# Dense-expert stages of a six-stage layer: score products by tile, gate steps later, waits per half pair, the norm's scaling on ScalarE

## The chip, the core and the metric

The kernel runs on one core of a Trainium2 chip. The metric is the device time of one execution in microseconds (us), lower is better. The median of three runs is 1315.05 us (1312.03 to 1316.84). One execution was profiled: its own time is 1315.12 us, and the span from its first to its last instruction 1313.3 us. Engines are named as in the profile: PE is TensorE (PEld its weight loads), DVE is VectorE, ACT is ScalarE, POOL is GpSimd, SP the engine that issues most DMAs.

## The reference, cut to what matters

The input x has 2 x 2048 rows of 256 numbers. Six residual stages follow each other: a routed mixture of 32 experts, a gated linear attention, the mixture again, then the three that matter here: a dense-expert stage, a recurrent stage, and the dense-expert stage again with the same weights.

```python
x = x + 0.5 * L0_ffn(layernorm(x)); x = x + L0_attn(layernorm(x)); x = x + 0.5 * L0_ffn(layernorm(x))
x = x + 0.5 * L1_ffn(layernorm(x), router_w, w1, w2, w3)
x = x + L1_attn(layernorm(x), ...)
x = x + 0.5 * L1_ffn(layernorm(x), router_w, w1, w2, w3)

# L1_ffn: 8 experts of width 64, each row goes to its best 2
scores = x @ router_w.T
top, chosen = top_k(scores, 2); weight = softmax(top)
y = sum over the 2 of weight * ((silu(x @ w1[e]) * (x @ w3[e])) @ w2[e])
```

## The kernel before, in words

x stays in SBUF throughout, as 32 tiles of 128 rows. A dense-expert stage (`ffn1`, L1673; it is built twice, as ffn1a and ffn1b) does all 8 experts for all rows, 8 x 64 = 512 hidden columns, and multiplies each expert's hidden values by a gate that is zero for the experts not chosen. It works on 8 blocks of 4 tiles (512 rows). For a block, in this order:

- **norm**: `Norm.dve_moments` (L210) takes means and variances of 4 tiles on VectorE, `Norm.pool` (L239) makes the reciprocal deviation on GpSimd, `Norm.dve_apply` (L221) subtracts the mean and scales on VectorE (L229), `turn` (L1972) transposes eight 128x128 pieces on PE (L262), and ScalarE copies the result twice, as f32 (`turned`, L1861) and as bf16 (`turned16`, L1867).
- **score** (L1924): the router's product in f32, 8 columns wide, four tiles in one run (the trace has 16 matmuls for it), then `keep_logits` (L1873) on ScalarE.
- **gates** on VectorE (L1754): parts 0 and 1 find the largest scores and their places, 2 and 3 the difference and the one-hot rows, two `tanh` on ScalarE (L1901) the softmax of two, parts 4 and 7 to 10 the gate values, split in two bf16 halves. PE transposes them (`gates`, L1934), ScalarE copies them (L1896).
- **up** (L1942): for each quarter m of the hidden columns a pair of products, x w1 into `ps_a` and x w3 into `ps_b`, each two matmuls of 512 columns in bf16. Each of the two has a single PSUM bank. `keep_ab` (L1879) evicts both on ScalarE: silu of the first (L1883), a copy of the second (L1884). One semaphore, `ab_made`, tells that both halves are made, and one, `ab_kept`, that both are evicted.
- **spread** (L1953) brings the gate values of a quarter over all its columns, into `ps_c`. `hidden` on VectorE (L1802) multiplies silu by b (part 0, product m) and the result by the gates (part 1, h m).
- **down** (L1960): the output products of a half block, 8 matmuls; `add` (L1816) adds them into x on VectorE.
- ffn1a alone also has `combine`, passed from the mixture ahead: for each block and half VectorE adds three tables from DRAM into x (L1148, L1151) ahead of the block's norm. In ffn1b SP stores a finished block to the output.

The engines run lists written out by hand, tied by semaphores. `staged` (L115) makes rounds; in one round five blocks are in work at different steps: j2, j1, j0, je and jy, each one block behind the one before. je is in its up products, jy in its down products, j1 in its norm. PE's list in a round is

```python
gates(je); up(je, 1); spread(je, 0); down(jy, 0); up(je, 2); spread(je, 1); turn(j1); up(je, 3)
spread(je, 2); down(jy, 1); score(j1); spread(je, 3); up(j0, 0)
```

VectorE's list (L1822) begins with half a combine and the moments of j1, then has for m = 0 to 3 product m, the gate parts of j0, h m, with the scaling of j1 after h 0, an add in m = 1 and m = 3, and half a combine of j2 in m = 2. ScalarE's (L1886) is keep_ab 0, keep_logits(j0), the copy of je's gates, keep_ab 1, keep_ab 2, the tanh of j0, turned(j1), keep_ab 3, turned16(j1).

Of the kernel before, what the change touches and what calls it, by code (L numbers as in the profile page):

```python
# [1672 lines left out]
def ffn1(nc, name, x, con, w, weights16, combine=None, x_out=None):  # L1673
# [7 lines left out]
    with Scope(nc, name) as sc:  # L1681
# [10 lines left out]
        if first_use:  # L1692
# [14 lines left out]
        silu = sc.sb("silu", [P, NM1, BN], BF16)  # L1707
        prod = sc.sb("prod", [P, 2, BN], BF16)
        h = sc.sb("h", [P, 2, NM1, BN], BF16)
        names = ("router_landed landed cast logits_made logits_kept xb_made g_step diff_made part_made split_made "  # L1710
                 "g_turned g_kept ab_made ab_kept prod_made c_made h_made y_made y_added stored")
        (router_landed, landed, cast, logits_made, logits_kept, xb_made, g_step, diff_made, part_made, split_made,
         g_turned, g_kept, ab_made, ab_kept, prod_made, c_made, h_made, y_made, y_added, stored) = (
             sc.sem(n) for n in names.split())
        ln.xT_users = [(logits_made, 1), (xb_made, 1)]
# [6 lines left out]
        with nc.Block() as block:  # L1722
# [18 lines left out]
            @block.gpsimd  # L1741
            def _(pool):
                ln.pool_start()
                each(pool, ln.pool, NB)

            @block.vector
            def _(dve):
# [73 lines left out]

                def work(j2, j1, j0, je, jy):  # L1822
# [26 lines left out]
                if combine:  # L1849
                    combine.dve(number(0), 0)  # L1850
                    combine.dve(number(0), 1)
                ln.dve(number(0), tile_of(number(0)))
                if combine:
                    combine.dve(number(1), 0)
# [3 lines left out]
            def _(act):  # L1858
                s = nc.scalar

# [6 lines left out]
                def turned16(j):  # L1867
                    b, p, i = j
                    act.wait_ge(ln.transposed, b + 1)
                    after(act, ab_made, NM1 * (b - 1))  # L1870
# [8 lines left out]
                def keep_ab(j, m):  # L1879
                    c = NM1 * j[0] + m  # L1880
                    act.wait_ge(ab_made, c + 1)
                    after(act, prod_made, c + 1 - NM1)
                    s.activation(silu[:, m], ps_a[:], ACT.Silu)  # L1883
                    s.activation(b16[:, m], ps_b[:], ACT.Copy).then_inc(ab_kept, 1)  # L1884

                def work(j2, j1, j0, je, jy):  # L1886
                    for m in range(NM1):
                        if je:
                            keep_ab(je, m)
                        if m == 0:  # L1890
                            if j0:
                                keep_logits(j0)
# [4 lines left out]
                        if m == 2:  # L1897
# [10 lines left out]
                s.preload_act_table_set(SILU)  # L1908
                if first_use:
# [6 lines left out]
                turned(number(0))  # L1916
                turned16(number(0))
# [3 lines left out]
            def _(pe):  # L1921
                mm = nc.tensor.matmul

                def score(j):  # L1924
                    b, p, i = j
                    pe.wait_ge(ln.xT_ready, b + 1)
                    after(pe, logits_kept, b)
                    for t in range(BT):
                        for k in range(KD):
                            ins = mm(ps_r[:, t * E1:(t + 1) * E1], ln.xT[:, p, k, t * P:(t + 1) * P], wr[:, k, :],  # L1930
                                     start=k == 0, stop=k == KD - 1)
                    ins.then_inc(logits_made, 1)
# [498 lines left out]
```

## Time and profile before

| | |
|---|---|
| median of three runs | 1315.05 us |
| the profiled execution | 1315.12 us |
| its span | 1313.3 us |
| mean granted clock of PE | 0.875 |
| busy share of the span: PE, DVE, ACT, POOL | 84%, 58%, 39%, 29% |
| ffn1a, first instruction to the last | 881.1 to 1020.6 us |
| ffn1b, first instruction to the end | 1186.8 to 1313.3 us |

The two stages together take about a fifth of the span. The rest of this text looks at their rounds. A round is counted from one start of the gate transposes on PE (L1939) to the next; there are eight such starts in a stage. The granted clock (PEclk) is the share of PE's full clock that the chip let through: 1.00 is 2.4 GHz and 0.50 is 1.2 GHz, and a value between them is a mean over a stretch. In a timeline an entry in brackets tells how long the engine stood idle before the row, and which engine ended that.

### The profile page before, as it was taken

The page shows a single profiled execution, that of the slowest core. Times are in us where ns is not written, and L with a number is a line of the kernel's source. Part 1 is how long each engine was busy: PE and PEld are TensorE (multiplying, and loading weights), DVE is VectorE, ACT ScalarE, POOL GpSimd, SP SyncE. Part 2 cuts the span into 40 slices and gives each one's busy share as a digit, 9 for nine tenths or more (in the row PEclk, how much of TensorE's full clock was granted, in tenths as well). Part 3 has the DMA queues.
Part 4 walks back from the last instruction along what each step waited for, and adds up shares of the span by engine and source line. Part 5 has one row for each costly group of instructions (what it writes and reads, how often), then busy time and mean ns, then how long its engine had stood idle before and what let it go on. Part 6 is the DMA issues. An engine that isn't in the chain of part 4 may idle for free. (4 is left out here: it accounts for less than half of the span.)

```text
span 1313.3 us, 17356 instructions
## 1 busy us (share of the span) xinstructions
PE 1100.3 (84%) x5232; PEld 676.8 (52%) x5252; DVE 765.7 (58%) x2655; ACT 512.3 (39%) x989; POOL 383.5 (29%) x414
## 2 busy tenths in 40 slices
PE   7999898938999688887999797936888399987896
PEld 5756565614444355556656565614444255543443
DVE  4596352216664466665597352216996399965775
ACT  5421232304556544435422222314444455523543
POOL 3003656640000233323003647541000246521100
PEclk7699998969999799996699998966778699996878
DMA  8655757663230000003655647764320100000001
GB/s 287 213 171 143 147 126 181 147 133 125 97 96 0 9 1 0 0 0 119 213 171 140 143 94 185 171 126 161 111 82 1 42 1 0 0 0 1 33 32 65
DMA packets 102872, 123.70 MB, mean 94 GB/s; under 512 B 17264, under 2 KB 97504, under 8 KB 100704
## 3 DMA queue, kind: packets, MB, share of 16 engines
q1 hardware_dynamic: 87440, 100.54, 23.2%
q0 software_dynamic: 15360, 22.29, 11.2%
q8 instruction: 33, 0.54, 0.2%
q14 instruction: 39, 0.32, 0.1%
HBM read 73.53 MB, written 50.07 MB: 94 GB/s over the span
## 5 line engine op out<-in xcount | busy, mean ns | idle before, releaser
L614 POOL DMA_INDIRECT ffn_sums<-ffn0b_xT,ffn0b_into x40 | 62.8, 1571 | 45.0 <-ACT ffn0b_xT L890 31.2
L614 POOL DMA_INDIRECT ffn_sums<-ffn0a_xT,ffn0a_into x40 | 63.0, 1574 | 43.4 <-ACT ffn0a_xT L890 20.2
L1488 POOL TENSOR_TENSOR attn_attend_state_m<-attn_attend_state,attn_attend_heads 128x512 f32<-128x512 f32 x15 | 24.3, 1619 | 97.0 <-DVE attn_attend_state L1520 66.3
L1148 DVE TENSOR_TENSOR main_spare<-main_spare 128x512 f32<-128x512 f32 x32 | 22.0, 686 | 52.2 <-DMA main_spare<-ffn_sums 52.1
L1644 PE MATMUL attn_attend_ps_w<-attn_attend_wo,attn_attend_y 128*128 128x256 f32 x128 | 31.9, 392 | 20.8 <-DVE attn_attend_y L1531 20.8
L739 PE MATMUL ffn0b_ps_b<-ffn0b_early,main_x 128*128 128x160 f32 x256 | 44.6, 322 | 3.9 <-ACT ffn0b_early L873 3.2
L739 PE MATMUL ffn0a_ps_b<-ffn0a_early,main_x 128*128 128x160 f32 x256 | 44.0, 318 | 3.4 <-ACT ffn0a_early L873 2.5
L1520 DVE SCALAR_TENSOR_TENSOR attn_attend_state<-attn_attend_state,attn_decay,attn_attend_ps_s 128x256 f32<-128x256 f32 x32 | 14.0, 478 | 54.8 <-PE attn_attend_ps_s L1629 54.8
L2319 PE MATMUL attn_ps_r<-attn_xr,attn_wr 128*128 128x512 f32 (+1 forms) x96 | 45.2, 593 | 0.7 <-DVE attn_out L2183 0.7
L2314 PE MATMUL attn_ps_k<-attn_xk,attn_wk 128*128 128x512 f32 (+1 forms) x96 | 45.6, 597 | 0.0
L739 PEld LDWEIGHTS ffn0b_ps_b<-ffn0b_early,main_x 128*128 128x128 f32 x256 | 39.7, 203 | 9.4 <-issue 3.8
L761 PE MATMUL ffn0b_ps_b<-main_x,ffn0b_h 128*32 128x256 f32 (+2 forms) x144 | 44.1, 407 | 0.3 <-issue 0.3
L2329 PE MATMUL attn_ps_y<-attn_wv,attn_out 128*128 128x256 f32 (+1 forms) x192 | 43.0, 379 | 1.2 <-DVE attn_out L2183 1.2
L761 PE MATMUL ffn0a_ps_b<-main_x,ffn0a_h 128*32 128x256 f32 (+2 forms) x144 | 43.8, 406 | 0.0
L739 PEld LDWEIGHTS ffn0a_ps_b<-ffn0a_early,main_x 128*128 128x128 f32 x256 | 39.0, 200 | 8.9 <-issue 4.1
L1644 PEld LDWEIGHTS attn_attend_ps_w<-attn_attend_wo,attn_attend_y 128*128 128x128 f32 x128 | 23.0, 189 | 36.1 <-DVE attn_attend_y L1531 20.3
L2329 PEld LDWEIGHTS attn_ps_y<-attn_wv,attn_out 128*128 128x128 f32 (+1 forms) x192 | 36.3, 189 | 10.1 <-issue 3.3
L1033 DVE TENSOR_TENSOR ffn0b_h<-ffn0b_sg,ffn0b_ps_b 128x160 f32<-128x160 f32 x32 | 10.3, 321 | 53.2 <-ACT ffn0b_sg L880 43.8
L1508 DVE COPY_PREDICATED main_spare<-attn_attend_causal,attn_attend_ps_a 128x1024 f32<-128x1024 int32 x32 | 39.8, 1296 | 2.5 <-issue 2.5
L1883 ACT ACTIVATE ffn1a_silu<-ffn1a_ps_a 128x512 bf16<-128x512 f32 x32 | 19.1, 596 | 56.5 <-PE ffn1a_ps_b L1949 53.5
L1033 DVE TENSOR_TENSOR ffn0a_h<-ffn0a_sg,ffn0a_ps_b 128x160 f32<-128x160 f32 x32 | 10.3, 321 | 51.5 <-ACT ffn0a_sg L880 42.9
L1883 ACT ACTIVATE ffn1b_silu<-ffn1b_ps_a 128x512 bf16<-128x512 f32 x32 | 19.1, 596 | 50.5 <-PE ffn1b_ps_b L1949 47.8
(450 smaller groups left out, 2880.4 us busy)
## 6 DMA issues: line engine op xcount, KB each, us to landing
main_x<-w_experts SPq DMA_DIRECT2D x16, 1536.0 KB, 6.8
main_spare<-ffn_sums SPq DMA_DIRECT2D x96, 256.0 KB, 3.5
ffn_sums<-main_x SPq DMA_DIRECT2D x32, 512.0 KB, 5.3
ffn_rows<-ffn0a_early SPq DMA_DIRECT2D x8, 512.0 KB, 5.8
ffn_sums<-ffn0a_zero SPq DMA_DIRECT2D x8, 512.0 KB, 7.0
ffn_rows<-ffn0b_early SPq DMA_DIRECT2D x8, 512.0 KB, 2.9
ffn_sums<-ffn0b_zero SPq DMA_DIRECT2D x8, 512.0 KB, 6.3
x_out<-main_x SPq DMA_DIRECT2D x8, 512.0 KB, 2.9
```

The costliest lines, as they stand in the source:

```text
L614: g.indirect_dma_start(out=sums[:, :], out_offset=IndirectOffsetOnAxis(ap=into[:, at, j:j + 1], axis=0), in_=ys[:, n % NY, :], in_offset=N ...
L739: ins = mm(ps_b[:, p, j * CAP:(j + 1) * CAP], we[:, r, n, j, k * F:(k + 1) * F], xgT[:, k, e // ME % 2, e % ME].rearrange("p a b -> p (a b)"),
L761: ins = mm(ps_b[row:row + m, 2 + piece % 2, 0:D], eh[:, p, at:at + m], we[:, r, n, 2, :], start=True, stop=True)
L1033: v.tensor_tensor(eh[:, p, :], esg[:, p, :], ps_b[:, p, CAP:2 * CAP], ALU.mult).then_inc(eh_made, 1)
L1148: v.tensor_tensor(self.parts[:, half, 0], self.parts[:, half, 0], self.parts[:, half, 1], ALU.add).then_inc(self.added, 1)
L1488: g.tensor_tensor(state_m[:], state[:], heads[:].unsqueeze(1).to_broadcast([P, 2, D]), ALU.mult).then_inc(s_masked, 1)
L1508: vec.copy_predicated(att[:, p, s].rearrange("p (r n) i -> p r n i", n=2), causal[:].unsqueeze(1).unsqueeze(1).to_broadcast([P, 4, 2, P]), ...
L1644: ins = mm(ps_w[:, s, :], y[:, k, s, :], wo[:, k, :], start=k == 0, stop=k == KD - 1)
L1883: s.activation(silu[:, m], ps_a[:], ACT.Silu)
L2314: ins = mm(ps_k[0:rows, m % 2], wk[:, k, at:at + rows], xk[:, p, k, :], start=k == 0, stop=k == KD - 1)
L2319: ins = mm(ps_r[0:rows, m % 2], wr[:, k, at:at + rows], xr[:, p, k, :], start=k == 0, stop=k == KD - 1)
L2329: ins = mm(ps_y[:, t, :], out[0:rows, p, m, t * P:(t + 1) * P], wv[0:rows, m, :], start=m == 0, stop=m == NMH - 1)
```

## The change

- **Score by tile.** `score(j, t)` does one tile. PE's list becomes: gates(je), up(je, 1), spread(je, 0), score(j0, 3), down(jy, 0), up(je, 2), spread(je, 1), turn(j1), up(je, 3), spread(je, 2), score(j1, 0), down(jy, 1), score(j1, 1), spread(je, 3), up(j0, 0), score(j1, 2).
- **Gates later.** The fourth score tile of a block lies in the next round, so the gate parts are done at m = 1 (0, 1), m = 2 (2, 3) and m = 3 (4, 7, 8, 9, then 10).
- **Waits per half pair.** `ab_made` becomes `a_made` and `b_made`, and `a_kept` is added beside `ab_kept`: silu waits for its own half, and the first product of the next pair waits for silu alone.
- **Scaling on ScalarE.** `apply` does it as one activation per tile with a scale and a bias per row; GpSimd makes the bias (minus mean times scale) with two more operations per block, and sets a tile of -1 at the start. In a round it comes after keep_logits and ahead of keep_ab(je, 1).
- **Moments earlier.** VectorE takes the moments of j2, after h 2, and the combine halves of j2 come after h 0 and h 2.
- At the start of ffn1a the first block's norm comes ahead of the casts of the weights on ScalarE.

```diff
@@ gpsimd
-                each(pool, ln.pool, NB)
+                def norm(j):
+                    b, p, i = j
+                    pool.wait_ge(ln.moments_ready, b + 1)
+                    g.tensor_tensor(ln.ve[:, p, :], ln.moments[:, p, :, 1], ln.eps[:], ALU.add).then_inc(ln.ve_ready, 1)
+                    after(pool, shift_ready, b)
+                    g.tensor_tensor(neg_mean[:], ln.moments[:, p, :, 0], minus[:], ALU.mult)
+                    pool.wait_ge(ln.ve_ready, b + 1)
+                    after(pool, ln.xn_ready, b - 1)
+                    g.tensor_tensor(ln.rstd[:, p, :], ln.ve[:, p, :], ln.power[:], ALU.pow).then_inc(ln.rstd_ready, 1)
+                    pool.wait_ge(ln.rstd_ready, b + 1)
+                    g.tensor_tensor(shift[:, p, :], neg_mean[:], ln.rstd[:, p, :], ALU.mult).then_inc(shift_ready, 1)
+                each(pool, norm, NB)
@@ vector
                 def work(j2, j1, j0, je, jy):
-                    if j1:
-                        if combine:
-                            combine.dve(j1, 1)
-                        ln.dve_moments(j1, tile_of(j1))
                     for m in range(NM1):
                         if je:
                             hidden(je, m, 0)
-                        if m == 0:
-                            if je:
-                                hidden(je, m, 1)
-                            if j1:
-                                ln.dve_apply(j1, tile_of(j1))
                         if j0:
-                            for n in ((0, 1), (2, 3), (4,), (7, 8, 9))[m]:
+                            for n in ((), (0, 1), (2, 3), (4, 7, 8, 9))[m]:
                                 gates(j0, n)
                         if m == 3 and jy:
                             add(jy, 1)
                         if m == 3 and j0:
                             gates(j0, 10)
-                        if je and m:
+                        if je:
                             hidden(je, m, 1)
                         if m == 1 and jy:
                             add(jy, 0)
-                        if m == 2 and j2 and combine:
+                        if m == 0 and j2 and combine:
                             combine.dve(j2, 0)
+                        if m == 2 and j2:
+                            if combine:
+                                combine.dve(j2, 1)
+                            moments(j2)
@@ scalar
+                def apply(j):
+                    b, p, i = j
+                    act.wait_ge(shift_ready, b + 1)
+                    after(act, ln.transposed, b - 1)
+                    for t in range(BT):
+                        ins = s.activation(ln.xn[:, p, t, :], x[:, tile_of(j)(t), :], ACT.Identity,
+                                           scale=ln.rstd[:, p, t:t + 1], bias=shift[:, p, t:t + 1])
+                    ins.then_inc(ln.xn_ready, 1)
                 def keep_ab(j, m):
                     c = NM1 * j[0] + m
-                    act.wait_ge(ab_made, c + 1)
+                    act.wait_ge(a_made, c + 1)
                     after(act, prod_made, c + 1 - NM1)
-                    s.activation(silu[:, m], ps_a[:], ACT.Silu)
+                    s.activation(silu[:, m], ps_a[:], ACT.Silu).then_inc(a_kept, 1)
+                    act.wait_ge(b_made, c + 1)
                     s.activation(b16[:, m], ps_b[:], ACT.Copy).then_inc(ab_kept, 1)
...
                         if m == 0:
-                            if j0:
-                                keep_logits(j0)
                             if je:
                                 act.wait_ge(g_turned, je[0] + 1)
                                 after(act, c_made, NM1 * je[0])
                                 s.activation(gate_t[:], ps_g[:, 0:BN], ACT.Copy).then_inc(g_kept, 1)
-                        if m == 2:
+                            if j0:
+                                keep_logits(j0)
+                            if j1:
+                                apply(j1)
+                        if m == 2 and j1:
+                            turned(j1)
+                        if m == 3:
                             if j0:
...
                             if j1:
-                                turned(j1)
-                    if j1:
-                        turned16(j1)
+                                turned16(j1)
@@ tensor
-                    after(pe, ab_kept, c)
-                    for ps, wt in ((ps_a, w1), (ps_b, w3)):
+                    for ps, wt, kept, made in ((ps_a, w1, a_kept, a_made), (ps_b, w3, ab_kept, b_made)):
+                        after(pe, kept, c)
                         for k in range(KD):
                             ins = mm(ps[:], wt[:, k, m * P:(m + 1) * P], xb[:, p, k, :],
                                      start=k == 0, stop=k == KD - 1)
-                    ins.then_inc(ab_made, 1)
+                        ins.then_inc(made, 1)
```

## Rows read from the trace of the kernel before

**Rows 1.** Stretches by round; columns: us, busy (count) of PE, PEld, DVE, ACT, POOL; PEclk; DMA.

```profile
908.62:922.51 13.89, 12.20 (x48) 5.89 (x48) 8.84 (x39) 6.89 (x14) 0.11 (x1) 0.62 0.12 40
951.80:966.38 14.58, 13.56 (x64) 6.84 (x65) 13.20 (x54) 6.48 (x15) 1.29 (x2) 0.73 0.33 103
995.09:1007.62 12.53, 10.37 (x42) 3.99 (x41) 6.98 (x34) 5.41 (x13) 0.00 (x0) 0.73 0.00 0
1203.90:1217.86 13.96, 12.44 (x48) 5.89 (x48) 7.97 (x38) 7.00 (x14) 0.00 (x0) 0.62 0.00 1
1231.35:1244.29 12.94, 11.24 (x64) 6.23 (x65) 11.24 (x51) 6.88 (x14) 1.29 (x2) 0.89 0.22 74
1285.59:1295.50 9.91, 7.62 (x42) 3.24 (x41) 6.88 (x34) 5.41 (x13) 0.00 (x0) 1.00 0.13 45
```

**Rows 2.** Stretches around one fall of the clock, same columns.

```profile
1255.20:1258.60 3.40, 3.10 (x23) 2.17 (x24) 3.06 (x11) 1.11 (x2) 0.00 (x0) 1.00 0.18 60
1258.60:1262.00 3.40, 2.60 (x7) 0.72 (x8) 1.44 (x9) 1.87 (x6) 1.29 (x2) 0.50 0.28 95
```

**Rows 3.** Waits in ffn1b, 1203.9 to 1295.5: who, for whom, us in total, times, longest.

```profile
PE ffn1b_ps_a L1949 <- ACT ffn1b_b L1884: 7.6, 9, 0.9
```

**Rows 4.** Timeline, PE, upper level: start us, us taken, engine, line, operation, out<-in, count.

```profile
1252.85 0.59 PE L1949 MATMUL ffn1b_ps_a<-ffn1b_xb,main_w 128*128 128x512 bf16 x2
...
1253.81 0.38 PE L1958 MATMUL ffn1b_ps_c<-ffn1b_gate_t,main_pick 16*128 16x512 bf16 x1
...
1254.12 1.05 PE L1968 MATMUL ffn1b_ps_y<-main_w,ffn1b_h 128*128 128x256 bf16 x8
...
1255.01 1.85 PE L1930 MATMUL ffn1b_ps_r<-ffn1b_wr,ffn1b_ln_xT 128*128 128x8 f32 x16
...
1258.07 0.39 PE L1939 MATMUL ffn1b_ps_g<-main_ident,ffn1b_split 128*16 128x128 bf16 x4
...
1259.40 1.03 PE L1949 MATMUL ffn1b_ps_a<-ffn1b_xb,main_w 128*128 128x512 bf16 x2 [0.94 <-ACT ffn1b_b L1884]
```

**Rows 5.** Timeline, ACT: scaling in the recurrent stage; evictions in ffn1b.

```profile
1042.09 2.06 ACT L2256 ACTIVATE attn_ln_xn<-main_x,attn_shift,attn_ln_rstd 128x256 f32<-128x256 f32 x4
...
1258.26 0.60 ACT L1883 ACTIVATE ffn1b_silu<-ffn1b_ps_a 128x512 bf16<-128x512 f32 x1 [2.29 <-PE ffn1b_ps_b L1949]
1258.75 0.59 ACT L1884 ACTIVATE ffn1b_b<-ffn1b_ps_b 128x512 bf16<-128x512 f32 x1
1259.23 0.20 ACT L1876 ACTIVATE ffn1b_logits<-ffn1b_ps_r 128x32 f32<-128x32 f32 x1
```

**Rows 6.** Timeline, DVE: scaling, gates, products and moments in ffn1b.

```profile
1234.68 1.38 DVE L229 TENSOR_SCALAR ffn1b_ln_xn<-main_x,ffn1b_ln_moments,ffn1b_ln_rstd 128x256 f32 x4
...
1235.98 0.16 DVE L1762 MAX8 ffn1b_top<-ffn1b_logits 128x8 f32<-128x8 f32 x1
...
1236.93 0.42 DVE L1809 TENSOR_TENSOR ffn1b_prod<-ffn1b_silu,ffn1b_b 128x512 bf16<-128x512 bf16 x1
...
1241.80 0.18 DVE L1799 TENSOR_TENSOR ffn1b_split<-ffn1b_gate,ffn1b_split 128x32 bf16<-128x32 f32 x1
...
1257.82 1.40 DVE L213 BATCH_NORM_STATS2 ffn1b_ln_stats<-main_x 128x6 f32 x4
...
1259.35 0.28 DVE L218 BATCH_NORM_AGGREGATE ffn1b_ln_moments<-ffn1b_ln_stats 128x2 f32<-128x6 f32 x3
```

**Rows 7.** Timeline, DVE: half a combine in a round of ffn1a.

```profile
947.91 0.68 DVE L1148 TENSOR_TENSOR main_spare<-main_spare 128x512 f32<-128x512 f32 x1
...
949.64 0.42 DVE L1809 TENSOR_TENSOR ffn1a_prod<-ffn1a_silu,ffn1a_b 128x512 bf16<-128x512 bf16 x1
```

**Rows 8.** Timeline, PE, lower level (ffn1a's round and ffn1b's fill).

```profile
953.31 1.06 PE L1949 MATMUL ffn1a_ps_b<-ffn1a_xb,main_w 128*128 128x512 bf16 x2
...
954.30 0.60 PE L1958 MATMUL ffn1a_ps_c<-ffn1a_gate_t,main_pick 16*128 16x512 bf16 x1
...
1198.67 3.58 PE L1930 MATMUL ffn1b_ps_r<-ffn1b_wr,ffn1b_ln_xT 128*128 128x8 f32 x16 [1.42 <-ACT ffn1b_ln_xT L1865]
```

More of the change, by code:

```diff
@@ L1707, in ffn1 @@
         silu = sc.sb("silu", [P, NM1, BN], BF16)
+        minus = sc.sb("minus", [P, BT])
+        neg_mean = sc.sb("neg_mean", [P, BT])
+        shift = sc.sb("shift", [P, 2, BT])
         prod = sc.sb("prod", [P, 2, BN], BF16)
         h = sc.sb("h", [P, 2, NM1, BN], BF16)
[L1710 to L1713, printed above, removed]
+        names = ("router_landed landed cast minus_set shift_ready logits_made logits_kept xb_made g_step diff_made part_made split_made "
+                 "g_turned g_kept a_made b_made a_kept ab_kept prod_made c_made h_made y_made y_added stored")
+        (router_landed, landed, cast, minus_set, shift_ready, logits_made, logits_kept, xb_made, g_step, diff_made, part_made, split_made,
+         g_turned, g_kept, a_made, b_made, a_kept, ab_kept, prod_made, c_made, h_made, y_made, y_added, stored) = (
              sc.sem(n) for n in names.split())
-        ln.xT_users = [(logits_made, 1), (xb_made, 1)]
         wide = [P, BT, E1]
@@ L1820, in add, with moments @@
                     v.tensor_tensor(rows, ps_y[:], rows, ALU.add).then_inc(y_added, 1)
+                def moments(j):
+                    ln.dve_moments(j, tile_of(j))
                 def work(j2, j1, j0, je, jy):
-                    if j1:
-                        if combine:
-                            combine.dve(j1, 1)
-                        ln.dve_moments(j1, tile_of(j1))
                     for m in range(NM1):
@@ L1845, in work @@
                             add(jy, 0)
-                        if m == 2 and j2 and combine:
+                        if m == 0 and j2 and combine:
                             combine.dve(j2, 0)
[L1849 to L1854, printed above, removed]
+                        if m == 2 and j2:
+                            if combine:
+                                combine.dve(j2, 1)
+                            moments(j2)
+                for b in range(2):
+                    if combine:
+                        combine.dve(number(b), 0)
+                        combine.dve(number(b), 1)
+                    moments(number(b))
                 staged(dve, work, NB)
@@ L1869, in turned16 @@
                     act.wait_ge(ln.transposed, b + 1)
-                    after(act, ab_made, NM1 * (b - 1))
+                    after(act, b_made, NM1 * (b - 1))
                     s.activation(xb[:, p], ps_t[:], ACT.Copy).then_inc(xb_made, 1)
@@ L1903, in work @@
                             if j1:
[L1904 to L1906 removed]
+                                turned16(j1)
                 s.preload_act_table_set(SILU)
+                act.wait_ge(ln.power_set, 1)
+                apply(number(0))
+                turned(number(0))
+                turned16(number(0))
                 if first_use:
@@ L1922, in _, with score @@
                 mm = nc.tensor.matmul
-                def score(j):
+                def score(j, t):
                     b, p, i = j
[L1926 to L1932, printed above, removed]
+                    if t == 0:
+                        pe.wait_ge(ln.xT_ready, b + 1)
+                        after(pe, logits_kept, b)
+                    for k in range(KD):
+                        ins = mm(ps_r[:, t * E1:(t + 1) * E1], ln.xT[:, p, k, t * P:(t + 1) * P], wr[:, k, :],
+                                 start=k == 0, stop=k == KD - 1)
+                    if t == BT - 1:
+                        ins.then_inc(logits_made, 1)
                 def gates(j):
@@ L1980, in work @@
                         spread(je, 0)
+                    if j0:
+                        score(j0, 3)
                     if jy:
@@ L1990, in work @@
                         spread(je, 2)
+                    if j1:
+                        score(j1, 0)
                     if jy:
@@ L1993, in work @@
                     if j1:
-                        score(j1)
+                        score(j1, 1)
                     if je:
@@ L1998, in work @@
                         up(j0, 0)
+                    if j1:
+                        score(j1, 2)
                 warm(nc, con, ps_t[:, 0, :], 5 if combine else 3)
@@ L2002, in _ @@
                 pe.wait_ge(router_landed, 16)
-                score(number(0))
+                for t in range(BT - 1):
+                    score(number(0), t)
                 if first_use:
```

5 lines of the change are left out of this document (3 added, 2 removed).

## The prediction

> **What bounds the kernel now.** Only the two dense-expert stages are touched, so I read them round by round, with the stretches view cut at the start of each round's gate transposes on TensorE (PE, L1939) [rows 1]. From the first to the seventh of these starts ffn1a takes 995.09 - 908.62 = 86.5 us and ffn1b 1285.59 - 1203.90 = 81.7 us; the seventh round takes 12.5 and 9.9. In a round of ffn1a VectorE is busy 13.20 of 14.58 us, so VectorE (DVE) is nearly the bound there. In ffn1b it is busy 11.24 of 12.94 in the round with the highest clock, and ScalarE (ACT) has half its time free: 6.88 us. The same view in short stretches shows the clock [rows 2]: PE runs at its upper level (1.00, 2.4 GHz) through 1255.20 to 1258.60, a stretch filled mostly by the narrow score matmuls, then waits, and the next stretch is at the lower level (0.50, 1.2 GHz). So a round has a mean granted clock of 0.62 to 0.89 [rows 1], and PE's own work takes long. Last, the waits: PE stood 7.6 us, nine times, for the copy of the second projection [rows 3], 0.94 us once in the timeline [rows 4].
>
> **What a round is afterwards.** I follow one round from the start G of its gate transposes, PE at the upper level. On PE come: transposes 0.39, expert pair 1 0.96 (1252.85 to 1253.81), spread 0 0.31, the fourth score tile 1.85 / 4 = 0.46 [rows 4]: 2.12 us. ScalarE has by then evicted what it could, but its list now reads: keep the logits, scale four tiles of the next block, and only then evict pair 1. The copy of logits takes 0.20, silu starts 0.49 before the copy of b, which takes 0.59 [rows 5]. The scaling does not exist in these stages; the same instruction on the same shapes, with a scale and a bias per row, stands in the recurrent stage: 2.06 us for four [rows 5]. I take that; below it the nearest row is VectorE's own 1.38 [rows 6], above it nothing longer than 4 x 0.60 = 2.4 (a silu of twice the columns, rows 5). So the pair is in SBUF at 2.12 + 0.20 + 2.06 + 0.49 + 0.59 = 5.46 us, and VectorE's product 1 waits for it. VectorE has done h 3, product 0 and h 0 by about 2.4, and in its list stands nothing else (in ffn1a half a combine): **some 3 us idle per round, where the scaling was meant to relieve it.**
>
> From product 1 on VectorE's list is unbroken. Its length can be read off: from product 1 to the end of the last gate step the round before does exactly these instructions in 1241.80 + 0.18 - 1236.93 = 5.05 us; added to them are gate parts 0 and 1, now behind product 1, 1236.93 - 1235.98 = 0.95, and the moments of the block two ahead, now behind h 2, 1259.35 + 0.28 - 1257.82 = 1.81 [rows 6]. Sum 7.81. The last gate step is what the next G waits for, so a round is at least 5.46 + 7.81 = **13.3 us in ffn1b**. In ffn1a half a combine stands behind h 2 as well, 949.64 - 947.91 = 1.73 [rows 7]: **15.0 us**. The round before with the highest clock was 12.94, and the usual one of ffn1a 14.58 [rows 1].
>
> **The parts, priced.** (1) VectorE loses 1.38 us of scaling per round [rows 6]; it buys nothing inside the chain, because the idle 3 us take its place. (2) The waits per half pair: silu can start a half pair earlier, and PE's next first half needs silu alone. In the rounds this is covered, since what is late next is ScalarE's scaling. PE after the fourth score tile and four output products (0.89 [rows 4]) is at 3.01, and pair 2 may start at 2.12 + 0.20 + 2.06 + 0.60 = 4.98: **PE stands 2.0 us**, against 0.94 before [rows 4]. It pays in the drain of a stage, where no scaling is queued: three waits of 0.9 [rows 3] fall to some 0.25 each, 2.0 us per stage, 4.0 in all. (3) The score tiles cost the same, 4 x 0.46, but lie between wide products. (4) GpSimd gets two small operations more per round; it is busy 1.29 of 14.58 us [rows 1], and the shift, started when the moments end, some 2.6 us ahead of G, is wanted 2.3 us behind it: cover of 3 us, cost nothing. SP issues the same loads and stores; the first half combine moves ahead of the gates of its round, so its next load starts earlier; nothing. (5) The fill of ffn1b: scaling costs 0.7 more than on VectorE (2.06 against 1.38) and waits for one more GpSimd operation, 0.3; and block 1's scaling now sits behind the last score tile of block 0, where VectorE did it beside the scores: about 1.6. Together +2.6, an estimate, bounds 1 and 4. In ffn1a the first block's turn no longer stands behind the weight casts, which gives the same amount back: 0, bounds -2 and +2.
>
> With the clock always at the upper level: round 1 has no output adds (12.1 and 13.8), rounds 2 to 5 are 13.3 and 15.0, round 6 has no moments but PE's own list and stand, 12; round 7 has no scaling, 9.7. ffn1b rounds 1 to 6: 12.1 + 53.2 + 12 = 77.3, -4.4; ffn1a: 13.8 + 60.0 + 12 = 85.8, -0.7; round 7: -0.2 and -2.8; fill +2.6, drains -4.0. Sum **-9.5 us**.
>
> **The clock.** Will it stay up? PE's list takes about 10 us of the 13.3. The thin stretches are now two: the fourth score tile and the stand of 2.0 with only output products between, and, at the round's end, the third score tile and a wait of 1.3 for the gates (PE is through at about 11.9). Before, one thin stretch (1.85 of scores, 0.94 of waiting [rows 4]) was enough to lose the upper level in nearly every round. I take it that the level still falls in most rounds. Where it falls ahead of the scaling, pair 1 takes 0.99 per half instead of 0.48, the tile 3.58 / 4 = 0.90 instead of 0.46 [rows 8]: chain +1.6, and both later spreads come late, up to 1.7 more. Where it falls behind the stand, pairs 2 and 3 make h 1 and h 2 late by 0.7 and 0.8: +1.5. With three rounds in ten spared I take +1.5 on average for the twelve rounds 1 to 6, +18, and +3 for the first rounds, which begin at the lower level (0.62 [rows 1]), and ffn1a's seventh. So -9.5 + 21 = **+11.5 us**. Most of it is in ffn1a, the rest in ffn1b.
>
> The profiled execution took 1315.12 us, 1.8 more than its span of 1313.3, and the median of three is 1315.05; the sum is made against the former: 1326.6.
>
> **Where a rule speaks otherwise.** VectorE is busy 91% of a ffn1a round [rows 1]. The Trainium skill (Perfetto Trace Analysis, Optimizing Scalar/DVE Operations) says that where VectorE is saturated, moving work to ScalarE may make sense. By that rule the 1.38 us would come off each of 14 rounds.
>
> **Rivals.** *The upper level holds.* For it: no narrow stretch is longer than 0.46 us, and rounds of the drain with waits of 0.9 ran at 1.00 (9.91 us, [rows 1]). Against it: the stand of 2.0. Time: the sum above, 1305.6. It decides if PE's stand after the first output products leaves the granted clock at 1.00. Chance 0.17.
> *The relief counts.* VectorE's list, not the wait behind the scaling, sets the round: 14 x 1.38 = 19.3 less, fill +2.6: 1298. It needs product 1 to be ready when h 0 ends; the order on ScalarE speaks against it. That is the result the page's rule would give. Chance 0.06.
> *Both halves cancel.* The level falls in every second round only and the wait costs 0.8 instead of 1.5: -9.5 + 10 = 1316. Chance 0.15.
> *The lower level stays.* PE stands a quarter of each round and is not given the upper level again: every product, transpose and tile doubles, and PE's list alone makes rounds of some 18 us: 12 x 4.5 = 54 more, -9.5 + 54 = +44.5, 1360. Against it: behind the stand lie some six microseconds of unbroken wide work, and the round [rows 1] always got the level back before. Chance 0.05.
> My forecast, slower by the queue on ScalarE with a clock that still falls: 0.57, own range 1318 to 1342.
>
> **How the numbers follow.** A measurement of this kernel tells about 0.5%, 6.6 us, from no change: 1308.5 to 1321.6. Faster: most of the first rival and the second, 0.17. Same: the rest of it, the third, and the low end of the forecast, 0.27. Slower: the rest, 0.56. The range 1304 to 1342 takes in the first rival and leaves out the second and fourth and the forecast's tail.
>
> **What would show it.** Right: VectorE's product waits for ScalarE's b some 3 us in each round; PE's first half of pair 2 waits about 2 us for silu; gate transposes wait for the split, VectorE; rounds of 14 to 15.5 us in ffn1b, 16 to 17.5 in ffn1a; PEclk still alternating; the drains 2 us shorter. Wrong: rounds under 13.3 and 15.0 (then the chain is misread), or PEclk at 1.00 throughout, or a wait of VectorE for DMA.

## The result and the profile after

The kernel after takes 1345.22 us (median of four, 1341.36 to 1350.33), the kernel before, run beside it, 1314.03: ratio 1.0235, 95% interval 1.019 to 1.028, **slower by some 31 us**. The forecast was 1326.6 and its range ended at 1342. The profiled execution took 1341.36 us. Its page, the clock line of the 40 slices included:

```profile
span 1337.5 us, 17455 instructions
...
PE 1106.0 (83%) x5252; PEld 684.8 (51%) x5252; DVE 745.0 (56%) x2591; ACT 548.4 (41%) x1053; POOL 388.7 (29%) x448
...
PEclk7699899969999799986799899766678699996788
```

The rounds in the stretches view, cut as in [rows 1]; columns: busy us of PE, its weight loads, VectorE, ScalarE, GpSimd, each with its instructions; then the granted clock, the DMA share, GB/s. First the six rounds of ffn1a and of ffn1b as one stretch each, then a middle and the seventh round of ffn1a and three rounds of ffn1b:

```profile
903.58:1011.67 108.09, 85.71 (x369) 46.19 (x368) 66.46 (x277) 54.82 (x109) 8.23 (x20) 0.68 0.19 59
1220.96:1311.74 90.78, 74.63 (x369) 42.14 (x368) 52.64 (x247) 54.71 (x109) 8.23 (x20) 0.77 0.07 24
...
959.01:978.51 19.50, 15.61 (x65) 8.16 (x65) 11.93 (x50) 9.31 (x18) 1.70 (x4) 0.66 0.25 80
1011.67:1021.08 9.41, 8.20 (x45) 3.57 (x44) 7.00 (x35) 5.50 (x13) 0.00 (x0) 1.00 0.01 2
1253.63:1268.64 15.01, 12.68 (x64) 7.27 (x65) 9.37 (x44) 9.20 (x18) 1.61 (x4) 0.77 0.11 37
1268.64:1281.98 13.34, 10.12 (x64) 6.05 (x64) 9.01 (x44) 9.09 (x18) 1.70 (x4) 1.00 0.12 39
1281.98:1298.03 16.05, 12.96 (x65) 7.18 (x65) 9.29 (x44) 9.31 (x18) 1.61 (x4) 0.79 0.10 33
```

VectorE has less work than before (11.9 busy in a round of ffn1a against 13.2 in [rows 1]) and the rounds are longer, 19.5 against 14.6. Six rounds of ffn1a took 86.5 us and take 108.1, of ffn1b 81.7 and 90.8. Over the two stages, each from its first instruction: ffn1a +18.5 (fill +0.6, six rounds +21.6, the seventh -3.1, drain -0.6), ffn1b +10.0 (fill +2.9, rounds +9.1, the seventh -0.5, drain -1.5). Between them the recurrent stage is 1.3 longer, and the unchanged stages ahead were 5.7 shorter in this execution. Together 24.2, the difference of the two spans (1337.5 and 1313.3).

Now the timeline of one round of ffn1b (start, length, engine, line, what it does; in brackets the idle time ahead and what ended it). It answers to [rows 4 to 6]:

```profile
1253.63 0.39 PE L1969 MATMUL ffn1b_ps_g<-main_ident,ffn1b_split 128*16 128x128 bf16 x4 [1.09 <-DVE ffn1b_split L1817]
...
1255.24 0.61 PE L1959 MATMUL ffn1b_ps_r<-ffn1b_wr,ffn1b_ln_xT 128*128 128x8 f32 x4
...
1255.89 0.20 ACT L1900 ACTIVATE ffn1b_logits<-ffn1b_ps_r 128x32 f32<-128x32 f32 x1 [1.24 <-PE ffn1b_ps_r L1959]
1256.13 2.08 ACT L1881 ACTIVATE ffn1b_ln_xn<-main_x,ffn1b_shift,ffn1b_ln_rstd 128x256 f32 x4
1258.11 0.58 ACT L1907 ACTIVATE ffn1b_silu<-ffn1b_ps_a 128x512 bf16<-128x512 f32 x1
1258.58 0.58 ACT L1909 ACTIVATE ffn1b_b<-ffn1b_ps_b 128x512 bf16<-128x512 f32 x1
...
1258.74 1.03 PE L1979 MATMUL ffn1b_ps_a<-ffn1b_xb,main_w 128*128 128x512 bf16 x2 [1.16 <-ACT ffn1b_silu L1907]
1259.19 0.43 DVE L1827 TENSOR_TENSOR ffn1b_prod<-ffn1b_silu,ffn1b_b 128x512 bf16<-128x512 bf16 x1 [3.16 <-ACT ffn1b_b L1909]
```

ScalarE ends its wait for the fourth score tile at 1255.89, copies the logits, scales for 2.08, and only then evicts pair 1, whose products were done before the tile. Product 1 starts 5.56 us after the gate transposes; VectorE had stood 3.16. The waits view of ffn1a's rounds (engine, line waited for; us in total, times, longest), to be read against [rows 3]:

```profile
DVE ffn1a_h L1832 <- PE ffn1a_ps_c L1988: 24.4, 18, 2.5
DVE ffn1a_prod L1827 <- ACT ffn1a_b L1909: 16.7, 8, 3.4
...
PE ffn1a_ps_g L1969 <- DVE ffn1a_split L1817: 13.4, 5, 2.8
...
PE ffn1a_ps_a L1979 <- ACT ffn1a_silu L1907: 8.9, 6, 2.8
```

The second and fourth lines are the forecast's waits. The first and third are its surprise in size: PE stands 2.7 us ahead of the gates in ffn1a, where before it stood once in six rounds, for 0.6; and VectorE waits again and again for a PE that runs mostly at its lower level, 24.4 us in 18 waits where before it waited 5.1 in 6.

### The profile page after: what moved, and what is told of

It reads as the page before. It is cut to its first block and busy times, and to the rows that moved or that the text cites. A ratio compares the mean times of both kernels' runs of the same rounds, so it can differ in the third digit from the quotient of the medians.

```text
span 1337.5 us, 17455 instructions
## 1 busy us (share of the span) xinstructions
PE 1106.0 (83%) x5252; PEld 684.8 (51%) x5252; DVE 745.0 (56%) x2591; ACT 548.4 (41%) x1053; POOL 388.7 (29%) x448
## 5 line engine op out<-in xcount | busy, mean ns | idle before, releaser
L614 POOL DMA_INDIRECT ffn_sums<-ffn0b_xT,ffn0b_into x40 | 62.9, 1572 | 45.0 <-ACT ffn0b_xT L890 19.7
L2210 DVE TENSOR_TENSOR_SCAN attn_st<-attn_keep,attn_carry,attn_kr 128x512 f32<-128x512 f32 (+1 forms) x24 | 33.1, 1381 | 7.9 <-ACT attn_kr L2311 7.8
L1832 DVE TENSOR_TENSOR ffn1a_h<-ffn1a_prod,ffn1a_ps_c 128x512 bf16<-128x512 bf16 x32 | 21.9, 685 | 27.3 <-PE ffn1a_ps_c L1988 27.2
```

Of the source, the lines that this page charges most:

```text
L614: g.indirect_dma_start(out=sums[:, :], out_offset=IndirectOffsetOnAxis(ap=into[:, at, j:j + 1], axis=0), in_=ys[:, n % NY, :], in_offset=N ...
L2210: v.tensor_tensor_scan(st[0:rows, m % 2], keep[0:rows, m:m + 1].to_broadcast([rows, BN]), kr[0:rows, m % 2], carry[0:rows, p, m:m + 1], AL ...
```

## Experiments

The times are medians, and the ratios are to runs of the kernel before beside them, with a 95% interval. What each is about: the queue on ScalarE (first, second, fourth, seventh), the clock (third, eighth, eleventh), the parts alone (fifth, sixth, ninth), the best of both (tenth, twelfth). Six rounds of a stage are quoted as one stretch each, ffn1a above, ffn1b below.

No edit touches what runs ahead of ffn1a. Yet ffn1a starts between 874.6 and 884.5 us in the fourteen profiled executions, so a time of the whole kernel carries some microseconds from there. The last column leaves them out: in the one profiled execution of each kernel, the time from ffn1a's first instruction to the end, which is the two dense-expert stages and the recurrent stage between them. The others of its executions have no trace, so how far that column varies by itself is not known.

| kernel | median | ffn1a starts | from there to the end |
|---|---|---|---|
| before | 1314.03 | 881.1 | 432.2 |
| after | 1345.22 | 875.5 | 462.0 |
| 1, scaling behind pair 1 | 1314.55 | 883.0 | 429.8 |
| 2, combine and moments first | 1311.33 | 874.6 | 428.3 |
| 3, both stands filled | 1319.9 | 880.8 | 441.2 |
| 4, both orders | 1293.7 | 877.9 | 413.5 |
| 5, waits alone | 1292.9 | 880.4 | 407.5 |
| 6, tiles alone | 1300.06 | 880.2 | 418.0 |
| 7, scaling on VectorE | 1313.84 | 882.3 | 431.1 |
| 8, fill ahead of pair 2 | 1331.17 | 879.9 | 451.8 |
| 9, waits and tiles | 1286.37 | 875.4 | 411.9 |
| 10, each stage its order | 1290.88 | 876.2 | 410.6 |
| 11, fill ahead of the gates | 1331.3 | 880.7 | 449.5 |
| 12, scaling on ScalarE on the ninth | 1300.17 | 884.5 | 417.0 |

**1. The scaling behind pair 1.** On the kernel after, ScalarE's work:

```diff
+                        if m == 1:
                             if j0:
                                 keep_logits(j0)
                             if j1:
                                 apply(j1)
```

> The changed kernel, with keep_logits and the scaling on ScalarE put behind the eviction of pair 1 (before that of pair 2). Queue theory (the scaling ahead of pair 1 makes VectorE idle 3 us and PE stand 2 us in each round): product 1 no longer waits, PE's wait for silu before pair 2 falls from 1.2 or more to under 0.5 us, the upper-level chain falls from 13.3 and 15.0 us to about 12 and 13.7 us, and the time to 1295 to 1315. Rival (the moments and the combine half behind h 2 are what makes the rounds long, the queue is covered): the round stays over 14.5 and 17, and the time within 0.5% of the changed kernel's 1345, 1338 to 1352.

1314.55 us, ratio 0.998 [0.9945, 1.0015]: 31 us less than after, the whole of its loss, for the place of five operations in one queue (the copy of the logits and four scalings). In the last column it is 32. PE still stands 2.7 us ahead of ffn1a's gates here, and the clock there is 0.72.

```profile
911.30:1005.69 94.39, 78.92 (x364) 45.62 (x369) 66.34 (x277) 55.63 (x109) 8.21 (x20) 0.72 0.22 68
1214.46:1288.28 73.82, 65.20 (x363) 39.66 (x368) 52.51 (x247) 54.49 (x109) 8.22 (x20) 0.87 0.09 29
```

**2. Combine and moments ahead of product 1.** On the kernel after, VectorE's idle 3 us are given work; a wait for the shift two blocks earlier comes with it.

```diff
-                        if m == 0 and j2 and combine:
-                            combine.dve(j2, 0)
-                        if m == 2 and j2:
+                        if m == 0 and j2:
                             if combine:
+                                combine.dve(j2, 0)
                                 combine.dve(j2, 1)
+                            dve.wait_ge(shift_ready, j2[0] - 1)
+                            v.memset(waiter[:], 0.0)
                             moments(j2)
```

> The changed kernel, with both combine halves and the moments of j2 on VectorE behind h 0 (m = 0), where it idles, instead of behind h 2. Queue theory: they fill the idle time, which is about 3 us; the chain behind product 1 loses 1.8 us in ffn1b and 3.5 in ffn1a, of which 2.1 come back in ffn1a since the three take longer than the idle time; rounds of about 12 and 13.6 us at the upper level, time 1297 to 1322. Rival (VectorE's list is not what the gates wait for; PE's list at the lower level is): gates no longer wait for the split, but the rounds shorten by less than 1 us, and the time is over 1330.

1311.33 us, ratio 0.9974 [0.995, 0.9998]. The profiled execution, at 1305.52, was the fastest of its ten. There ffn1a gained most: six rounds fell from 108.1 to 83.8.

```profile
903.21:987.02 83.81, 66.28 (x364) 38.17 (x369) 65.71 (x282) 54.75 (x109) 8.07 (x20) 0.89 0.24 76
1197.26:1276.60 79.34, 65.77 (x364) 38.99 (x369) 53.44 (x252) 54.24 (x109) 8.51 (x20) 0.88 0.08 27
```

**3. PE's two stands filled.** On the kernel after, six wide products of no use ahead of the gate transposes and eight ahead of pair 2, in the rounds that have both blocks:

```diff
+                    if je and j0:
+                        pe.wait_ge(xb_made, j0[0] + 1)
+                        fill(6)
                     if je:
                         gates(je)
...
                         down(jy, 0)
+                    if je and j0:
+                        fill(8)
                     if je:
                         up(je, 2)
```

> The changed kernel, with matmuls that compute nothing needed (512 columns, bf16, into the free transpose bank) put in PE's two stands: 6 ahead of the gate transposes, 8 ahead of pair 2. It prices the clock by itself. Clock theory (rounds over 13.3 and 15.0 us are the lower level's doing): granted clock at 1.00 in nearly all rounds, rounds of 13.3 to 14 in ffn1b and 15.0 to 15.7 in ffn1a, time 1306 to 1320. Rival (the excess is something else, such as waits that the chain left out): the clock rises, the rounds stay at 15 and 18, time over 1335. A third way: the filler is late itself, lengthens PE's list at the lower level, and the time rises.

1319.9 us, ratio 1.0038 [1.0017, 1.0059].

```profile
910.15:1000.53 90.38, 80.63 (x445) 44.75 (x453) 66.13 (x277) 54.32 (x108) 8.24 (x20) 0.94 0.22 70
1214.97:1294.94 79.97, 76.95 (x445) 42.47 (x452) 51.90 (x247) 54.32 (x108) 8.24 (x20) 0.99 0.09 30
```

PE does more and the kernel is 25 us faster than after. Cut at the gates, rounds 2 to 5 of ffn1b are 13.4 each at a clock of 1.0, those of ffn1a 15.0 at 1.00 and 16.0 at 0.89: the chain without the clock, 13.3 and 15.0, was read rightly. The fall of the clock costs the kernel after some 25 us or more (21 by the last column), since the fill takes time too (the seventh rounds grow by 1.3 each). Ahead of ffn1a's gates the six products fill only part of the stand: 1.4 to 1.5 us of 2.7 are left.

**4. Both orders (1 and 2) at once.**

> The edits of e1 and e2 together. Queue theory: the edits treat the same idle time, so they do not add up: with nothing idle VectorE's list (some 10 us in ffn1b, 13.2 in ffn1a) and PE's list of 10 set the round: 11 to 12.5 and 13.5 to 14.5 us, time 1285 to 1308, below the kernel before. Rival (each removes a stand of its own): the gains against the changed kernel add up. If the clock keeps falling in each round, both gains shrink and the time stays over 1315.

1293.7 us, ratio 0.9818 [0.9768, 0.9868].

```profile
906.30:995.81 89.51, 79.65 (x363) 46.59 (x368) 65.87 (x282) 55.85 (x109) 8.06 (x20) 0.72 0.23 71
1204.88:1266.08 61.20, 57.52 (x363) 36.03 (x369) 51.82 (x252) 53.66 (x109) 8.07 (x20) 0.99 0.11 35
```

In ffn1b PE is busy 57.5 of 61.2 us: it hardly stands, and the clock stays up. ffn1a did not follow (89.5 at 0.72): there VectorE does both halves of a combine and the moments ahead of product 1, and PE's spreads wait for h, 8.0 us in five waits. That order on VectorE alone is not the cause: the tenth has it too, and its ffn1a took 83.1. Why the two orders together do badly in ffn1a stays open.

**5. The waits per half pair alone**, on the kernel before. ScalarE's half is shown; PE waits for `a_kept` ahead of a pair's first product and for `ab_kept` ahead of its second.

```diff
-                    act.wait_ge(ab_made, c + 1)
+                    act.wait_ge(a_made, c + 1)
                     after(act, prod_made, c + 1 - NM1)
-                    s.activation(silu[:, m], ps_a[:], ACT.Silu)
+                    s.activation(silu[:, m], ps_a[:], ACT.Silu).then_inc(a_kept, 1)
+                    act.wait_ge(ab_made, c + 1)
```

> The kernel before with the waits per half pair alone; score tiles in one run, scaling, gates and moments on VectorE as before. Prediction: in the rounds nothing, because silu's half pair is covered there; only the drains lose PE's stands for the copy of b, 2.0 us per stage, so about -4 us against before, and after's own drains (12.4 in both stages against 13.0 and 13.8) ask for -2. A rival, that the waits also shorten PE's stand of 0.94 in each round and with it save the upper level: 12 rounds x 0.5 or more, 1300 to 1308 us and PEclk at 1.00 in more rounds than one.

1292.9 us, ratio 0.9838 [0.9807, 0.9869]: 21 us, and I had given the part 4. The rival on record was nearer, and still too small: it gave 1300 to 1308.

```profile
907.35:990.32 82.97, 70.72 (x363) 38.34 (x368) 73.74 (x301) 42.45 (x84) 6.58 (x11) 0.82 0.26 81
1195.07:1264.06 68.99, 61.45 (x364) 35.41 (x369) 60.07 (x271) 40.99 (x84) 6.58 (x10) 0.94 0.10 32
```

Beside the kernel before, whose clock over these six rounds was 0.71 and 0.75, PE's stand of 0.9 behind the scores is gone and the clock is 0.82 and 0.94. So the part acts in the rounds. In ffn1b's six rounds before, those stands were 5.7 us, and the rounds are 12.7 shorter: the rest goes with the clock.

**6. The score tiles alone**, on the kernel before, all four within the same round:

```diff
+                    if j1:
+                        score(j1, 0)
                     if jy:
                         down(jy, 1)
                     if j1:
-                        score(j1)
+                        score(j1, 1)
                     if je:
                         spread(je, 3)
+                    if j1:
+                        score(j1, 2)
                     if j0:
                         up(j0, 0)
+                    if j1:
+                        score(j1, 3)
```

> The kernel before with its score products dealt out one tile at a time between wide work of the same round; everything else as before. If the run of 1.85 us of narrow products is what loses the upper level in the round before, the clock stays at 1.00 in most rounds and the rounds shrink to VectorE's own list, 12.5 to 13 us: some 1300 us. If the stand of PE is enough by itself, the clock stays at 0.7 to 0.75 and the time within 5 us of before. I take the second, 0.6 to 0.4, since the gates now wait longer: the last tile, and with it the logits, comes later by the tiles' distance.

1300.06 us, ratio 0.9884 [0.9851, 0.9916]. My bet lost again: the tiles cost the same and win 14 us.

```profile
907.43:994.23 86.80, 74.86 (x364) 42.76 (x369) 73.55 (x301) 42.20 (x85) 6.78 (x11) 0.77 0.26 78
1201.65:1271.72 70.07, 64.85 (x363) 37.77 (x369) 59.50 (x271) 41.33 (x85) 6.59 (x10) 0.89 0.09 31
```

**7. The scaling back on VectorE**, on the kernel after, behind h 0:

```diff
+                        if m == 0 and j1:
+                            ln.dve_apply(j1, tile_of(j1))
...
                                 keep_logits(j0)
-                            if j1:
-                                apply(j1)
```

> The kernel after with the four scaling operations back on VectorE, behind h 0, and nothing else changed (GpSimd still makes the shift, unused). My account of the round says that pair 1 is then in SBUF at 2.12 + 0.20 + 0.49 + 0.59 = 3.4 and VectorE, through with h 0 at 2.4, scales until 3.8, so the chain is 3.8 + 7.81 = 11.6 us in ffn1b and 13.3 in ffn1a, 1.7 less than after per round: 13 x 1.7 = 22 less, and PE's stand ahead of pair 2 falls from 2.0 to some 0.3, so the clock gives back more: 1305 to 1318 us. If the loss of after were in the later gates and moments, or in the score tiles, and not in the scaling's place on ScalarE, the time stays over 1335.

1313.84 us, ratio 0.9989 [0.9967, 1.0011], in the range given. The first block's scaling goes back with the others. Two rounds of ffn1b at a clock of 0.98 and 1.00 took 11.5 and 11.4 us, where the chain says 11.6. ffn1a stays at 0.72: its first five rounds are 15.8 to 17.0, not 13.3, and PE still stands 2.7 to 2.9 ahead of the gates.

```profile
908.49:1004.40 95.91, 80.39 (x362) 46.27 (x369) 73.65 (x301) 42.69 (x84) 8.65 (x22) 0.72 0.22 69
1209.31:1287.70 78.39, 70.47 (x364) 41.52 (x369) 59.85 (x271) 42.41 (x85) 8.21 (x20) 0.81 0.08 27
```

**8 and 11. One stand filled at a time**, on the kernel after: experiment 3 with the eight products ahead of pair 2 alone, and with the six ahead of the gates alone.

> The kernel after with eight wide products of no use ahead of pair 2, in the rounds of both stages, and none ahead of the gate transposes (the earlier run had both). It tells which stand loses the upper level. If the stand of 2.0 ahead of pair 2 is what loses it, PEclk is 1.00 or nearly in ffn1b with rounds of 13.4, and ffn1a at 15 to 16: 1320 to 1326. If the stand ahead of the gates (1.1 in ffn1b, 2.7 in ffn1a) loses it too, ffn1b is as with both and ffn1a keeps 0.7 and rounds of 17 to 18: about 1333. If the gates' stand is the cause in both stages, the time stays at 1340 or more.

> The kernel after with six wide products of no use ahead of the gate transposes, and none ahead of pair 2: the counterpart of the run with those ahead of pair 2 alone (1331.2), both together gave 1319.9. If either stand alone is enough to lose the upper level, the two halves of the fill do not add up to the whole: 1330 to 1342 here, ffn1a with rounds of 16 to 19 and a clock of 0.7 to 0.8. If the two stands' costs add, 1345 - (25 - 14) = 1334, with rounds of 16.5 in ffn1a. If the gates' stand was the larger part of it in ffn1a (2.7 us there), ffn1a's clock is over 0.85 and its rounds are near 15.5: about 1330 with ffn1b still at 15 to 16.

1331.17 us, ratio 1.0119 [1.0083, 1.0154], and 1331.3, 1.0118 [1.0068, 1.0167]: each 14 of the 25 us, but in different stages. First the former, then the latter:

```profile
908.29:1010.91 102.62, 88.09 (x410) 48.06 (x416) 66.42 (x277) 53.95 (x109) 8.23 (x20) 0.77 0.20 62
1221.53:1305.50 83.97, 76.30 (x410) 43.15 (x416) 52.24 (x247) 53.93 (x109) 8.24 (x20) 0.89 0.08 26
```

```profile
910.27:1003.11 92.84, 71.33 (x399) 40.67 (x405) 65.81 (x277) 54.60 (x108) 8.24 (x20) 0.93 0.22 68
1214.75:1304.41 89.66, 75.68 (x398) 42.55 (x404) 52.53 (x247) 55.08 (x108) 8.24 (x20) 0.87 0.08 28
```

With the gates' stand filled in part (1.4 to 1.5 of 2.7 us are left) ffn1a goes from 0.68 to 0.93 and loses 15.3 us of 108.1; with pair 2's filled it loses 5.5. In ffn1b it is the other way: 1.1 against 6.8. With pair 2's filled, three rounds of ffn1b ran at 1.00 with stands of 1.1 to 1.3 us ahead of the gates. The eleventh run also has a round of ffn1a whose clock was 1.00 throughout, with the other stand in it (stretches, then PE's timeline):

```profile
926.77:941.97 15.20, 11.38 (x69) 6.49 (x70) 11.74 (x50) 9.09 (x18) 1.91 (x6) 1.00 0.34 109
```

```profile
932.20 0.60 PE L1979 MATMUL ffn1a_ps_a<-ffn1a_xb,main_w 128*128 128x512 bf16 x2 [2.29 <-ACT ffn1a_silu L1907]
```

So a stand of 2.29 us ahead of pair 2, with one of 1.50 ahead of the gates, did not lose the level in that round. It took 15.20, where the chain says 15.0.

**9. Both parts that won alone** (5 and 6 together, on the kernel before).

> The kernel before with both parts that won alone: waits per half pair (-21 us against before) and score tiles dealt out one at a time within the round (-14). If both work through the same thing, a clock that stays up once the thin stretch of narrow products and standing is shorter, they cannot add in ffn1b, whose rounds are near 11 us in both and at 0.90 to 1.00: 1285 to 1293 us. If they are independent, -35: 1279. If the tiles' distance delays the logits and so the gates, which the faster rounds now show: 1295 or more. I take the first. What is left between this kernel and the one with the scaling back on VectorE (1313.8) is then the price of the later gates and moments: 20 to 28 us.

1286.37 us, ratio 0.9785 [0.973, 0.984]: the fastest median of the study. They do not add, as expected. That the tiles add anything to the waits is not shown: the interval overlaps the fifth's, and from ffn1a on this execution took 411.9 us, the fifth's 407.5. Against the seventh (1313.8, scaling on VectorE in both) 27 us are left, 19 from ffn1a on. What differs is the later gates, the place of the moments and of the combine halves, the tiles split over two rounds, the order of ScalarE's copies and GpSimd's shift. These were not parted.

**10. Each stage its order.** As the fourth, but in ffn1a the scaling ahead of pair 1 (`if m == (0 if combine else 1):`).

> The kernel with moments first and scaling behind pair 1 (1293.7 us), but in ffn1a the scaling ahead of pair 1 again, as in the run with moments first alone, whose ffn1a took 28.6 + 93.2 + 11.6 = 133.4 us against 138.9 here. If stages are independent, 1293.7 - 5.5 = 1288. If ffn1a's difference was luck of the clock's falls, 1290 to 1298.

1290.88 us, ratio 0.9813 [0.9745, 0.9882]; six rounds of ffn1a are 83.1 against 89.5, but the medians differ by less than their spread, so inconclusive.

**12. The scaling on ScalarE again, on the ninth.**

```diff
                                 hidden(je, m, 1)
-                            if j1:
-                                ln.dve_apply(j1, tile_of(j1))
...
+                        if m == 1 and j1:
+                            apply(j1)
```

> The kernel with half-pair waits and score tiles (1286.4 us; gates and moments where before had them) with the scaling moved to ScalarE, behind pair 1, GpSimd's shift with it. VectorE is busy 32.8 of 36.0 us in three rounds of ffn1b there, PE 33.0 of 36.0. If the relief of 1.38 us counts while nothing waits behind the scaling, up to 14 x 1.38 = 19 less, but PE is as busy as VectorE, so I expect about a third to a half of it: 1277 to 1281 us. If PE's list is the bound by now, no change: 1284 to 1290. If the transposes of the scaled block, now behind pair 1's eviction, the shift and 2.06 us of scaling, come late and leave a stand of PE ahead of them: 1290 or more, with PE's transposes waiting for ScalarE's scaling by over 1 us per round.

1300.17 us, ratio 0.9889 [0.9866, 0.9913], 14 more than the ninth: in the median the third outcome on record, with its wait (here in ffn1a):

```profile
PE ffn1a_ps_t L262 <- ACT ffn1a_ln_xn L1885: 10.4, 4, 3.1
```

Here the moments come at the head of the round, ScalarE waits for GpSimd's shift, and the transposes wait for ScalarE. But the wait does not account for 14 us. Of the 14.2 between the two profiled spans 9.1 lie ahead of ffn1a, in stages that the edit does not touch. Six rounds of ffn1a took 2.4 more than the ninth's, those of ffn1b 1.5 less, at a clock of 0.99. From ffn1a on it is 5.1 more. So the relief of VectorE brings no gain in all, and what the move costs here is not settled.

## Why the prediction was wrong, step by step

The sign and the mechanism held, the size did not: +31 by the medians where +11.5 was given. In the profiled execution the two stages together took 28.5 more, 17 above the sum, and the points below are about these 17.

- **The chain held.** G to product 1: 5.46 given, 5.56 measured; from there to the next G 7.81 given, and 7.79 in the round at 1.00 (1274.19 to 1281.98), which took 13.34 where 13.3 stood. VectorE waited 3.16 for b (some 3 given). Four scalings took 2.08 (2.06 given). The Trainium skill's rule on a saturated VectorE (Perfetto Trace Analysis, Optimizing Scalar/DVE Operations) did not come true here, in the change or in experiment 12: VectorE was relieved in both, and neither kernel was faster for it.
- **The edges held roughly.** Fill of ffn1b +2.9 (+2.6 given), of ffn1a +0.6 (0 given), seventh rounds 9.4 (9.7). The drains gave 2.0 together, not 4.0. Round 6 was given 12 and takes 13.2 at 1.00 (experiment 11): 2.4 more over both stages, hidden in the next point's number.
- **The failed step is the clock's +1.5 per round, +21 in all.** Six rounds were to take 85.8 and 77.3 at the upper level and took 108.1 and 90.8: 22.3 and 13.5 more, 35.8 in all. The error is 14.8 us, 11.8 of it in ffn1a if the 21 are shared evenly between the stages. I had worked out PE's wait for the gates once, for a round of 13.3 (1.3 us), and used it for ffn1a as well, whose round of 15.0 leaves PE through at 11.9 and standing 3. Measured were 2.7. The level then falls ahead of the gates, and both costs that I took as alternatives come in the same round: in that of 959.01 (PE's own timeline)

```profile
959.01 0.59 PE L1969 MATMUL ffn1a_ps_g<-main_ident,ffn1a_split 128*16 128x128 bf16 x4 [2.73 <-DVE ffn1a_split L1817]
...
965.87 1.04 PE L1979 MATMUL ffn1a_ps_a<-ffn1a_xb,main_w 128*128 128x512 bf16 x2 [1.24 <-ACT ffn1a_silu L1907]
...
969.99 1.06 PE L1979 MATMUL ffn1a_ps_a<-ffn1a_xb,main_w 128*128 128x512 bf16 x2
...
974.48 0.60 PE L1979 MATMUL ffn1a_ps_a<-ffn1a_xb,main_w 128*128 128x512 bf16 x2
```

  The two products of a first half take 1.04 from pair 1 to pair 3, and 0.60 only 15 us into the round. Product 1 starts 7.32 in (966.33, VectorE's timeline), 1.9 later than the chain, and h 1 and h 2 wait 0.60 and 2.03 more for a slow PE: 4.5 above 15.0, not 1.5. Experiment 11 shows it: with about half of that stand filled ffn1a ran at 0.93 and gave 15.3 us back.
- **"Three rounds in ten spared" was too many**: no round of ffn1a was at 1.00 before the seventh, and one in six of ffn1b.
- **The waits per half pair** were priced at 4 us, in the drains, and the drains gave 2.0. What the waits are worth in the rounds of the change was not measured. Alone they are worth 21 (experiment 5), the tiles within one round 14 (6), both 28 (9). The rest of the change costs 59 from there by the medians, 50 from ffn1a on in the profiled executions: 27 (19) for the later gates and what else differs between the ninth and the seventh, 31 (31) for the scaling ahead of pair 1 on ScalarE (7 to after).
- **The rivals.** The upper level did not hold (0.68 and 0.77). I hung it on pair 2's stand; in ffn1a the gates' stand weighed more (15.3 us against 5.5). Cancelling and relief fell. "The lower level stays" gave rounds near 18 us: ffn1a came to 18.1 to 19.7 in four of its rounds. I priced that case for both stages together, and not for one.

## What to carry to other kernels

An operation moved to an engine with half its time free costs nothing only if what stands behind it in that engine's queue can wait; the same five operations one place later were worth 31 us. Where TensorE's clock follows its stands, work out each stand for each stage by itself: in ffn1b's six rounds waits per half gave 12.7 us (81.7 to 69.0) for stands that sum to 5.7 there (7.6 with the seventh [rows 3]). Try the parts of a change alone: here two of them give 1286 us, and the rest takes twice that gain back.

## What was not expected of the hardware

- Products of no use made the kernel faster: 14 more of them per round, 25 us less (experiment 3).
- The level is not lost by the length of one stand alone: 2.29 us left it at 1.00 (experiment 11), while the kernel before lost it at a stand of 0.94 behind 1.85 us of narrow products [rows 2, 4]. In the kernel after two rounds of ffn1b follow each other with the same list and the same stands, 1.17 and 1.99 us, then 1.22 and 2.00 (first row ahead of the gates, second ahead of pair 2, in each round). The first kept the level, the second lost it over its second stand: its pair 2 takes 1.04 instead of 0.60. What decides stays open.

```profile
1268.64 0.39 PE L1969 MATMUL ffn1b_ps_g<-main_ident,ffn1b_split 128*16 128x128 bf16 x4 [1.17 <-DVE ffn1b_split L1817]
...
1273.74 0.60 PE L1979 MATMUL ffn1b_ps_a<-ffn1b_xb,main_w 128*128 128x512 bf16 x2 [1.99 <-ACT ffn1b_silu L1907]
...
1281.98 0.39 PE L1969 MATMUL ffn1b_ps_g<-main_ident,ffn1b_split 128*16 128x128 bf16 x4 [1.22 <-DVE ffn1b_split L1817]
...
1287.09 1.04 PE L1979 MATMUL ffn1b_ps_a<-ffn1b_xb,main_w 128*128 128x512 bf16 x2 [2.00 <-ACT ffn1b_silu L1907]
```

- The same list on PE fares differently in two stages: in the fourth experiment the rounds of ffn1b ran at 0.99, those of ffn1a, where VectorE has the combine besides, at 0.72.
